# Rows of x in two buffers up to chunk 23, and the scaling of Q's weights cut into eight steps, in an eight-core layer kernel

## What is computed

```
mod = (silu(c) @ wmod).reshape(4, 6, 1, -1)
sa, ca, ga, sb, cb, gb = (mod[:, i] for i in range(6))
ga, gb = sign(g) * max(|g|, 0.25)
h = layernorm(x) * (1 + ca) + sa
K, V, Q = h @ theta_K.T, h @ theta_V.T, h @ theta_Q.T
for each token:   g = 2/1024 * (W @ k + b - v)
                  W = W - 0.01 * outer(g, k);  b = b - 0.01 * g
                  out = W @ q + b
x = x + ga * out
h = layernorm(x) * (1 + cb) + sb
x = x + gb * (shared_ffn(h) + sum of the 2 routed experts of 8, by softmax(h @ router_w))
```

## Time and profile before

| what | us |
|---|---|
| three runs | 1603.39, 1615.85, 1644.12; median 1615.85 |
| the profiled execution | 1616.92, its slowest core (3) with a span of 1615.3 |
| spans of the even cores (0, 2, 4, 6) | 1535.8, 1546.6, 1536.4, 1550.9 |
| spans of the odd cores (1, 3, 5, 7) | 1612.0, 1615.3, 1609.5, 1596.2 |
| busy on core 3: PE, DVE, ACT, POOL | 1417.2, 738.8, 493.8, 304.0 |
| shares of the chain that ended last: PE, DMA, DVE, issue | 71%, 13%, 8%, 5% |

### The profile page before, as it was taken

One profiled execution on the slowest core, in us unless ns is written; L12 is line 12 of the kernel. 1 busy time (PEld: TensorE's weight loads), 2 busy tenths in 40 slices (PEclk: granted clock), 3 DMA queues, 4 the chain that ended last, 5 costly groups with the idle time before them and its releaser, 6 DMA issues.

```text
span 1615.3 us, 22747 instructions; the slowest of 8 cores (1535.8 to 1615.3 us)
## 1 busy us (share of the span) xinstructions
PE 1417.2 (88%) x7825; PEld 703.9 (44%) x7825; DVE 738.8 (46%) x1278; ACT 493.8 (31%) x784; POOL 304.0 (19%) x209
## 2 busy tenths in 40 slices
PE   0587899798968998999997899999797999989897
PEld 0343444344444444444543444644343444434354
DVE  2426555647444456457447423432122222222576
ACT  1144444345444444444434321122121111101010
POOL 0058875803300001001011110000000000000131
PEclk9999999899989999999998999999899999999999
DMA  9954356616457522122172659397999999974763
GB/s 238 265 114 136 105 151 125 156 53 169 85 131 137 157 66 92 53 92 76 43 170 92 169 126 239 105 221 146 213 194 210 170 202 224 180 157 173 272 209 131
DMA packets 82373, 244.16 MB, mean 151 GB/s; under 512 B 7365, under 2 KB 7493, under 8 KB 77638
## 3 DMA queue, kind: packets, MB, share of 16 engines
q0 software_dynamic: 47440, 112.75, 35.2%
q1 hardware_dynamic: 26870, 92.05, 17.2%
q10 hardware_dynamic: 7936, 37.75, 9.5%
HBM read 262.46 MB, written 78.64 MB: 211 GB/s over the span
## 4 chain that ended last, share of the span: by engine, by line
PE 71%; DMA 13%; DVE 8%; issue 5%; POOL 1%; ACT 1%; another core or an unknown queue 1%; SPq 0%; DVEq 0%; POOLq 0%; ACTq 0%
PE prep L664 9%; PE u L928 7%; PE gate L897 5%; PE u L826 5%; PE up L897 5%; PE up L894 5%; PE gate L894 5%; PE prep L928 4%; PE up L729 3%; PE up L756 3%; DMA w1u<-uw 3%; PE gate L729 3%; DMA w1u<-suw 3%; PE gate L746 2%; DMA wmb<-wmod 2%
## 5 line engine op out<-in xcount | busy, mean ns | idle before, releaser
L1416 DVE TENSOR_TENSOR act<-up,sgb 128x512 bf16<-128x512 f32 (+1 forms) x128 | 84.0, 658 | 317.1 <-PE up L897 194.6
L1084 ACT ACTIVATE sgb<-gate 128x512 bf16<-128x512 f32 (+1 forms) x128 | 73.0, 570 | 466.1 <-PE gate L897 228.2
L1292 DVE TENSOR_TENSOR WT<-WT,u 128x512 f32<-128x512 f32 x240 | 153.4, 679 | 52.3 <-PE u L826 52.0
L826 PE MATMUL u<-Gsb,Ktk 128*128 128x512 bf16 x480 | 129.7, 394 | 41.9 <-DVE WT L1292 40.8
L664 PE MATMUL prep<-hft,s_thK 128*128 128x512 bf16 x512 | 124.3, 391 | 7.5 <-ACT hft L993 3.4
L1054 ACT CAST Wbf<-WT 128x1024 bf16<-128x1024 f32 x120 | 124.7, 1041 | 14.7 <-DVE WT L1292 14.6
L1603 POOL DMA_INDIRECT hx<-h2m,sl x28 | 29.1, 1038 | 447.4 <-DVE sl L1399 441.8
L826 PEld LDWEIGHTS u<-Gsb,Ktk 128*128 128x128 bf16 x480 | 44.0, 100 | 99.5 <-issue 63.9
L1545 POOL TENSOR_SCALAR x2b<-x2b,silc 128x1024 f32<-128x1024 f32 x28 | 80.1, 2862 | 23.6 <-DMA x2b<-wmod 22.5
L664 PEld LDWEIGHTS prep<-hft,s_thK 128*128 128x128 bf16 x512 | 50.5, 100 | 72.2 <-issue 18.9
L746 PE MATMUL gate<-Wbf,Kft 128*128 128x512 bf16 x256 | 80.8, 391 | 0.0
(11 more groups left out here) (250 smaller groups left out, 2318.2 us busy)
## 6 DMA issues: line engine op xcount, KB each, us to landing
hx<-zero ACTq DMA_DIRECT2D x4, 5120.0 KB, 30.6
x2b<-wmod POOLq DMA_DIRECT2D x32, 512.0 KB, 5.1
yx<-ring SPq DMA_DIRECT2D x32, 512.0 KB, 5.9
xb<-x SPq DMA_DIRECT2D x22, 512.0 KB
wmb<-wmod SPq DMA_DIRECT2D x8, 1024.0 KB, 12.1
x2b<-x SPq DMA_DIRECT2D x16, 512.0 KB, 4.6
hx<-zero ACTq DMA_DIRECT2D x4, 2048.0 KB, 11.4
pair<-gw POOLq DMA_DIRECT2D x4, 2048.0 KB, 29.2
```

The source lines that it names most:

```text
L826: m = t.matmul(U[jh][:, 0:512], Ktk[s % 2][:, cc * D + dt * P:cc * D + (dt + 1) * P], Gsb[:, cc * D + jh * 512:cc * D + (jh + 1) * 512], s ...
L1292: v.tensor_add(w, w, U[jh][:, 0:512]).then_inc(S["v_W"], 1)
L1416: v.tensor_mul(act[k % 2][:, fj * ACW:fj * ACW + COLS[k]], R[2 + n % 2][:, 0:COLS[k]], sgb[n % 2][:, 0:COLS[k]]).then_inc(v_act, 1)
```

## The change

Two edits.

1. `x_slot` gives slot 1 to the odd chunks from 4 to 23 on an odd core, instead of 4 to 17. On an even core (`NPRE` = 0) it gives slot 0, as before.
2. The eight multiplications of `thQ` leave the step `qcol` and become eight steps `qs`, each of which signals `v_thQ`; the reader waits for 8. On an odd core four of them stand in super 4 (`fill[1]`, `[2]`, `[5]`, `[7]`) and four in super 5 (`fill[1]`, `[2]`, `[4]`, `[7]`). On an even core they stand right behind `qcol`, where they were.

```diff
@@ build_schedule
-        out += [("qcol",)] + row(0, 4)
+        out += [("qcol",)] + [("qs", dt) for dt in range(DT)] + row(0, 4)
...
         if NPRE and s == 3:
             fill[5] += [("qcol",)]
+        if NPRE and s in (4, 5):
+
+            for i in range(4):
+                fill[(1, 2, 5, 7)[i] if first else (1, 2, 4, 7)[i]] += [("qs", 4 * (s - 4) + i)]
@@ signals
-        "qcol": ["p_qc", "v_qc", "v_thQ"],
+        "qcol": ["p_qc", "v_qc"], "qs": ["v_thQ"],
@@ x_slot
-            return 1 if g % 2 and 4 <= g < NPRE else 0
+            return 1 if NPRE and g % 2 and 4 <= g < NPRE + 6 else 0
@@ tensor_prog
-                         "kw": lambda: t.wait_ge(ld_vb, 16), "q": lambda: t.wait_ge(S["v_thQ"], 1),
+                         "kw": lambda: t.wait_ge(ld_vb, 16), "q": lambda: t.wait_ge(S["v_thQ"], DT),
@@ vector_prog
-                        for dt in range(DT):
-                            m = v.tensor_scalar_mul(thQ[:, dt * D:(dt + 1) * D], thQ[:, dt * D:(dt + 1) * D],
-                                                    cac[:, dt:dt + 1])
-                        m.then_inc(S["v_thQ"], 1)
+                    elif kind == "qs":
+                        dt = arg[0]
+                        v.tensor_scalar_mul(thQ[:, dt * D:(dt + 1) * D], thQ[:, dt * D:(dt + 1) * D],
+                                            cac[:, dt:dt + 1]).then_inc(S["v_thQ"], 1)
```

More of the change, by code:

```diff
@@ L216, in signals @@
         "ht": ["p_ht", "a_ht"], "er": ["p_er", "v_er", "v_nmx", "a_ex", "v_mk"], "es": ["p_es", "v_es", "v_slot"],
-        "bc": ["p_bc", "v_bc"], "vrow": ["p_vr", "p_vr", "a_vr", "a_vr", "v_thV"], "qcol": ["p_qc", "v_qc", "v_thQ"],
+        "bc": ["p_bc", "v_bc"], "vrow": ["p_vr", "p_vr", "a_vr", "a_vr", "v_thV"], "qcol": ["p_qc", "v_qc"], "qs": ["v_thQ"],
         "cols": ["p_col", "v_col"] + DT * ["p_kc"] + ["v_kc", "v_thK"],
```

## The result

The changed kernel takes 1586.39 us (median of four runs: 1584.75, 1591.51, 1588.04, 1581.10), the kernel before 1610.81 us in the same comparison. The ratio is 0.984, with a 95% interval of 0.9806 to 0.9874: about 1.6% faster, and inside 2%. The medians lie 24.4 us apart. The forecast was 1589 us. Now and then an execution is some per cent longer, with a lower granted clock on the cores of one die; the medians in this text are over all runs, the ratios and their intervals leave such runs out.

A forecast was written before the change was run, and what follows sets the result against it. The odd cores bound the kernel, with PE idle in super 3 and at late rows of chunks 21 and 23. 9.65 - 1.8 + 13.4 + 6.3 = 27.5 us takes 1616.92 to 1589.4 us; forecast 1589, range 1573 to 1606.

The forecast's parts named there:

- Part 1 in super 3: Super 3, odd cores: without the multiplications the adds start 6.90 us sooner and 2.75 us of clock loss returns; gain 9.65 us.
- The clock's term: Super 3, 296.20 to 304.30 us: PE is busy at a mean clock of 0.66; the 2.75 us lost there come back.
- The eight in supers 4 and 5: The moved multiplications cost 1.0 us in super 4 and 0.8 in super 5, together 1.8; bounds 0 and 20.6 us.
- an idle time of that size leaves the clock alone: Super 3: the 1.07 us of PE idle time left lowers no clock, judged by 2.10 us of it in super 5.
- Part 2, chunk 21: Its load goes out about 45 us earlier; the 11.09 us stop and 2.3 us of clock loss go: 13.4 us.
- Chunk 23: Loaded after `xn` 21, 28 us before it is needed; its 4.06 us stop and 2.3 us of clock go: 6.3 us.
- Chunk 22: Its load takes 15.13 us and lands at 460.1, needed at 461.9: 1.8 us to spare, no cost counted.
- The shift lasts unless a shared resource takes it back: After 510 us loads, zeros and expert weights follow PE's progress, so the 27.5 us gained before stay gained.
- the first rival: Expert stage: an earlier start shortens PE's waits for weights, core 3 ends 7 us sooner still, 1582 us; chance 0.26.
- The third: Rival: expert stage bound by weights; three more waits (36 us) make the kernel slower, all six give 1661 us; chance 0.03.
- more than three sets of weights wait: Expert stage: one of the signs that would show the forecast wrong; three of the nine sets waited before the change.

The follow-up runs named there:

- quiet POOL: The changed kernel without POOL's products and sums for the last row of `wmod` on the odd cores; 1590.09 us in one run.
- the variant with super 6: The changed kernel with the second four multiplications in super 6 instead of 5, each group at steps 2, 5, 6 and 7; 1589.28 us, ratio 0.9849.
- the place of chunk 21 alone: The kernel before with slot 1 for odd chunks up to 21 on the odd cores and nothing else changed; 1601.31 us in one run.
- the repeat: The changed kernel itself, measured once more on the same chip as a yardstick; 1584.89 us, ratio 0.9798 against the kernel before.

## Why the prediction was right, and where its steps were not

**Part 1 in super 3.** Predicted 9.65 us, measured 7.57 on core 3. The adds came up as said, but I counted 1.07 us of idle time left where there were 0.80 + 0.94 + 0.81 = 2.55 us: 1.48 us of the missing 2.08. With a quiet POOL the stretch takes 9.97 us, 1.07 less than the 11.04 of the changed kernel: that much is the `xn` which POOL holds up. The eight multiplications had hidden the following small waits for DVE, and the term for these was zero in my sum. The clock's term stood on a real effect (0.66 before, 1.00 after) and was nearly right. PE's work behind the idle time, from the first matmul of `u` on, ends where these matmuls begin, before and after:

```profile
304.30 0.59 PE L746 MATMUL gate<-Wbf,Kft 128*128 128x512 bf16 x2
```

```profile
293.58 0.59 PE L750 MATMUL gate<-Wbf,Kft 128*128 128x512 bf16 x2
```

That is 304.30 - 296.22 = 8.08 us without idle time before, and 293.58 - 286.22 - 0.94 - 0.81 = 5.61 us of work after: 2.47 us came back, for 2.75 in the sum. The 0.3 us that are left lie ahead of the idle time: from the copy to `qb`, where the stretch is cut, PE works 1.00 us in the kernel before and 1.31 in the changed one.

**The eight in supers 4 and 5.** Predicted 1.0 + 0.8 = 1.8 us. Super 4 cost nothing on core 3 though a multiplication there took 1.99 us, and the quiet-POOL run puts POOL's part at 0 to 1.3 us by core. Super 5 cost 0.76 for 0.8 where the clock stayed up, which the variant with super 6 confirmed. On the mean it costs more, by a term that the sum had at nothing. Without multiplications PE's idle time behind the adds to `b_f` in super 5 is 1.42 us, and on none of 24 odd cores (six kernels) did the clock fall there; with them it is 1.78 us, and on 9 of 28 (seven kernels) the granted clock fell to 0.50 behind it. Super 5 took 42.8 us on the mean of the 24 and 44.2 on that of the 28. The sentence "an idle time of that size leaves the clock alone" was read from one row: behind the 2.10 us of the earlier trace rows the clock fell on 26 of these 52 cores, on core 5 of the kernel before too, where the four matmuls still took 1.02 us and the granted clock was 0.60 from 382.1 to 385.7 us. In super 3 it held: 1.00 after the change. A blocked one that shows in full, 1.94 us, was met only where it was moved to another step.

**Part 2, chunk 21.** Predicted 13.4 us (11.09 + 2.3), measured 13.43 on core 3. The load was early, and that removes the stop whatever the zeros do: super 7 took 42.96 to 42.98 us in every kernel with chunk 21 in the second place, and 43.4 to 56.4 in those without.

**Chunk 23: right amount, wrong cause.** Predicted 6.3 us "Chunk 23 is loaded after `xn` 21", measured 6.34. But with 23 back in `xb` nothing is lost in super 8. That stop was a consequence of the first: the stop at 21 held core 3 back until its next zeros met core 2's (478.55 and 474.55), just as 23 was loaded. Without it (the place of chunk 21 alone) they are at 461.91 and 477.40, 15 us apart. I had counted two independent waits.

**Chunk 22.** The margin of 1.8 us rested on a load of 15.13 us. It took 6.8 us:

```profile
xb<-x SPq DMA_DIRECT2D x1, 512.0 KB, 6.8
```

and has no wait on any core. A load time that was measured inside a coincidence was carried to a place where the coincidence is gone, on this core. Where it stays, the thin margin is real: with the place of chunk 21 alone, core 4's zeros are 4.2 us ahead of core 5's, and core 5's load of chunk 22 goes out at 447.59 us and takes 16.4 us; it lands at 464.0, and the moments begin at 464.43. That nothing waited was in part luck. By the same mistake I treated the parts as additive: alone they give 29.3 us, together 24.3.

**The expert stage.** "The shift lasts unless a shared resource takes it back" holds on the mean: 7.2 us more were gained in the first profile, and 4.1 in that of the repeat (663.2 to 659.1). But by core it goes either way, 13.7 us shorter on core 3 and 2.2 longer on core 7. It goes roughly with the waits for weights: before, 19.6, 23.2, 18.8 and 15.6 us of waits go with stages of 664.3, 666.0, 663.1 and 659.2 us (cores 1, 3, 5, 7); after, 13.4, 12.4, 13.0 and 18.4 us with 658.1, 652.3, 652.1 and 661.5. So the first rival, that an earlier start shortens the waits, came out on cores 1, 3 and 5 and failed on core 7. Across kernels the start alone does not set the stage: in six kernels whose odd cores come to it at 918.5 to 921.4 us on the mean it took 656.0 to 662.4 us, and with the place of chunk 21 alone, from 927.1 us on, 666.0, against 663.2 from 945.1 before. So how much of the 7.2 us is the change's and how much the scatter of an execution stays open. The third, "the expert stage is bound by weights", had a true core, that weights are waited for, and a wrong premise, that the core's own engines are at their limit: the waits go when the even cores load less. The 36 us more of waits that it saw follow from an earlier start did not come: in both profiles of the changed kernel no core waits over 19.6 us in all. One sign of being wrong that I had named did show, "more than three sets of weights wait": on core 3 five did, on cores 5 and 7 four. It was a poor sign, since on core 3 the five waits are 12.4 us where the three before were 23.2.

**The total.** Up to the first own output core 3 gained 26.6 us for 27.5, and the kernel's median is 1586.4 for 1589. The first is the mechanism; that the second lies so close is in part luck. The sum was made on core 3, whose span fell by 44.2 us, and the slowest core is now core 7, at 1583.2, about where I had seen it come out (1585); that the four would lie close together was wrong, with core 3 at 1571.1. The 17.6 us that core 3 gained beyond the 26.6, most of it in the expert stage, did not reach the kernel's time, because core 7 gained only 13.0 in all.

## What to carry to other kernels

A wait for a load in a timeline says that the load was late, not why: look up what the other core of the pair writes at that moment before you buy a buffer, and do not carry the load's duration to another place. Stops in one chain are not independent: remove the first in an experiment of its own and see which others go with it, since the gains of parts were not additive here, and the second place was worth nothing for one of its two chunks. When small work moves out of a long block, count the short waits that the block had covered. A clock that stays up behind an idle time in one row of one core says little: look at the same place on all cores and in all traces.

## What the runs showed of the hardware

- Zeros of 5 MB written by both cores of a pair at once land in 38.0 us on one of them, and rows of 512 KB loaded meanwhile take 15.1 and 19.6 us. With the even core's zeros over 40 us away the same zeros land in 21.0 to 22.4 us, and the rows of chunk 21 in 4.4 and 5.3 us (cores 7 and 5); in the changed kernel core 3's zeros are 10.6 us ahead of core 2's (411.93 and 422.52), and the rows of chunk 22 took 6.8 us.
- PE's waits for expert weights on the odd cores, 12.4 to 23.2 us, fell to 0 to 1.1 us when only the even cores loaded less, and nothing in the odd cores' loads was changed. A DMA share of 1.05 and one of 1.01 stand for quite different amounts of waiting. The Trainium skill ("Perfetto Trace Analysis", section "Identifying the Most-Contended Engine") calls the occupancy of the 16 DMA engines misleading; this case agrees, with these two shares.
- A DVE multiplication of 0.48 us that starts inside a POOL sum of two tiles ends 0.27 to 0.28 us after it (1.99 and 2.43 us). In a POOL product with a column, of 2.85 us, it hangs on the start: 1.26 us into it the multiplication took 0.48 us, 2.40 us into it 0.73 us, ending 0.29 us after the product.
- PE's clock fell behind idle times of 1.78 us (9 of 28 cores) and 2.10 us (26 of 52), to a granted 0.50, the level of 1.2 GHz, and stayed up behind 1.42 us (24 of 24), all in super 5 of odd cores. At full clock the super takes 42.3 to 42.5 us without multiplications in it and 43.1 to 43.3 with them; with such a fall it takes up to 45.8 us, with POOL quiet too (45.5 us on core 3, where the granted clock is 0.83 over the 10 us from 350 to 360 us). Why on some cores only, with the same instructions, is open: no experiment was made on it.
